# Scatter of expert rows by accumulating DMA, with the routing weights stored beside the gathered rows

## The chip, the cores and the metric

The kernel runs on one core of a Trainium2 chip. The metric is the device time of one execution in microseconds (us), as the median of several runs. The profile comes from one further execution that the hardware profiler recorded. Engines: PE multiplies matrices (PEld is its weight load), DVE, ACT and POOL work on vectors, SP only issues DMAs here; ACT and POOL issue DMAs too.

## What is computed

The input is 8 sequences of 1,024 tokens of 256 values, 8,192 tokens in all. After a layer norm, one branch is a diagonal linear recurrence and the other a mixture of 8 experts, of which each token uses its best two.

```python
xn = _layernorm(x, axis=-1)
# recurrence: h_t = A * h_{t-1} + (xn_t B_w^T + B_b), A = sigmoid(log_A)
s = einsum('btn,dn->btd', h, C_w) + C_b
# experts
logits = einsum('bsh,he->bse', xn, Wr) + br
routing_weights, expert_indices = top_k(logits, 2)
routing_weights = softmax(routing_weights, axis=-1)
c = sum(one_hot(expert_indices, 8) * routing_weights[..., None], axis=-2)
h = silu(einsum('bsh,ehi->besi', xn, W1)) * einsum('bsh,ehi->besi', xn, W3)
y = einsum('besi,eih->besh', h, W2)
g = silu(einsum('bse,besh->bsh', c, y))
out = x + s * g
```

Inputs and result are float32.

## The kernel before

Engines run their own programs and meet at semaphores; the order on each is the order of the code, with no scheduler. There are 64 token tiles of 128 rows (TILES) in 16 chunks of 4 (CHUNKS, CT).

**Head (0 to about 155 us).** SP loads x chunk by chunk (L261). DVE, POOL and ACT normalise, PE transposes, and SP stores the normalised rows to the DRAM tensor xn_rows (L264), one row of 256 floats per token. PE computes router logits. DVE then finds the best two experts of each token (L677 to L683, top2_ready). Meanwhile PE makes the input products of the recurrence, called bx, two halves per chunk (make_bx, L979), and ACT moves each from its PSUM bank to h_sb (keep_bx, L450). There are four banks, so PE's half m of chunk c waits until the half two chunks earlier has been moved: bx_ready >= 2c + m - 3, that is both halves of chunk c-3 and the first of chunk c-2 for m = 0. ACT's program before chunk 3 also holds the sigmoid of log_A (L455) and the exp of the difference of the two logits, called ratio (L457), each with a table load. Between products PE makes ranks (L989, L990), edge transposes (L995), a histogram (L1001) and prefix sums; DVE turns them into slots, and 128 one-hot pairs (L731, L732) are multiplied on PE (L1019) into tables that give for each of 18,176 expert slots its token. The tables become gather_idx and scatter_idx (L749 to L763). DVE also makes weight1 = 1 / (1 + ratio) (L717, L718). SP loads the first expert's weights at the end of chunk 2 (L276), and ACT splits them into a high part from 140 us on (L491).

**Middle (to about 800 us).** 71 tiles of 256 slots, sorted by expert. For each tile POOL gathers 2 x 128 rows of xn_rows by an indirect DMA (L366, a ring of four tiles), PE transposes them (L1036), ACT and DVE split them into a high and a low part (L517, L781), PE multiplies (L1047 to L1049 and L1077, L1078), ACT and DVE do silu, product and splits, ACT copies the low half of y (L531), DVE adds it to the high half (L799), and POOL scatters the 256 rows to y_rows (L373), one row per token and choice, 16,384 rows in all. POOL's program alternates: gather tile i+4, scatter tile i. Slots that hold no token are skipped by an index out of bounds. In the first 32 tiles DVE also runs the recurrence's scans (L840).

**Tail (800 us on).** For each chunk SP loads the rows of the first and of the second choice (L287, two DMAs of 512 KB, a ring of four chunks), DVE mixes them (mix, L880: ratio x second + first), ACT applies silu with the scale weight1 (L586), PE has computed the output states of the chunk into two banks of S_BANKS (L1118 the bias, L1122 the products; four chunks of banks), DVE multiplies (apply, L891) and adds x (add_x, L898), and SP stores (L291). The DVE order is mix(g), apply(g-1), add_x(g-2). SP starts loading when the last scatter has landed.

## Time and profile before

| | us |
|---|---|
| median of 3 runs | 879.77 (879.41 to 879.9) |
| profiled execution | 880.07 |
| its span, first to last instruction | 878.3 |
| mean granted TensorE clock | 0.979 |

Busy shares are means over the whole span; what a stage is worth is read from timelines of that stage. In the timelines of the profile a row has the start, the length, the engine, the line of the kernel, what is written from what, the number of instructions merged into the row, and in brackets the idle time before it with the one that ended it. An engine's name with a q (SPq, ACTq) marks a row of the issuing queue, above all a DMA's issue. Landing is when all of the DMA's completions had arrived. A granted clock of 1.00 is 2.4 GHz, 0.50 is 1.2 GHz.

### The profile page before, as it was taken

The page shows a single profiled execution, that of the slowest core. Times are in us where ns is not written, and L with a number is a line of the kernel's source. Part 1 is how long each engine was busy: PE and PEld are TensorE (multiplying, and loading weights), DVE is VectorE, ACT ScalarE, POOL GpSimd, SP SyncE. Part 2 cuts the span into 40 slices and gives each one's busy share as a digit, 9 for nine tenths or more (in the row PEclk, how much of TensorE's full clock was granted, in tenths as well). Part 3 has the DMA queues.
Part 4 walks back from the last instruction along what each step waited for, and adds up shares of the span by engine and source line. Part 5 has one row for each costly group of instructions (what it writes and reads, how often), then busy time and mean ns, then how long its engine had stood idle before and what let it go on. Part 6 is the DMA issues. An engine that isn't in the chain of part 4 may idle for free.

```text
span 878.3 us, 17926 instructions
## 1 busy us (share of the span) xinstructions
PE 815.5 (93%) x5608; PEld 730.3 (83%) x5608; DVE 521.3 (59%) x1149; ACT 395.5 (45%) x768; POOL 321.5 (37%) x345
## 2 busy tenths in 40 slices
PE   2579994899999999999999999999999999998994
PEld 2444442899999999999999999999999999997883
DVE  5837896446575665655655443545554553543998
ACT  3664674334454443434544443434444543432443
POOL 3420402244444444444453534444444534421000
PEclk9989998899999999999999999999999999999997
DMA  9942002112141321112222311112332211203998
GB/s 297 322 161 72 1 0 75 58 57 65 54 129 51 102 82 60 60 54 66 96 89 81 101 54 60 60 54 75 111 106 79 62 59 60 60 16 110 360 384 296
DMA packets 65982, 90.78 MB, mean 103 GB/s; under 512 B 7646, under 2 KB 53219, under 8 KB 65956
## 3 DMA queue, kind: packets, MB, share of 16 engines
q1 hardware_dynamic: 51092, 54.80, 18.6%
q0 software_dynamic: 13632, 35.41, 12.9%
q10 hardware_dynamic: 1232, 0.28, 0.2%
q8 instruction: 9, 0.15, 0.1%
q14 instruction: 17, 0.14, 0.1%
HBM read 56.90 MB, written 35.39 MB: 105 GB/s over the span
## 4 chain that ended last, share of the span: by engine, by line
PE 87%; DVE 7%; issue 3%; ACT 2%; DMA 1%; DVEq 0%; ACTq 0%
PE bank L1047 16%; PE bank L1049 16%; PE bank L1048 16%; PE bank L1077 15%; PE bank L1078 8%; PE bank L979 5%; PE bank L1122 5%; PE bank L1036 3%; DVE stats L610 2%; PE bank L939 2%; DVE g_sb L880 1%; PE bank L1019 1%; ACT xnT L402 1%; PE bank L949 1%; DVE x_sb L898 1%
## 5 line engine op out<-in xcount | busy, mean ns | idle before, releaser
L1047 PE MATMUL bank<-xh,W_sb 128*128 128x256 f32 x1136 | 322.6, 284 | 3.0 <-DVE xl L781 3.0
L1049 PE MATMUL bank<-xl,W_sb 128*128 128x256 f32 x1136 | 322.1, 284 | 0.0
L1048 PE MATMUL bank<-xh,W_sb 128*128 128x256 f32 x1136 | 322.1, 284 | 0.0
L373 POOL DMA_INDIRECT y_rows<-y_sb,scatter_idx x142 | 145.2, 1022 | 326.0 <-DVE y_sb L799 302.7
L787 DVE TENSOR_TENSOR hbuf<-hbuf,bank 128x512 f32<-128x512 f32 x142 | 97.7, 688 | 239.7 <-PE bank L1049 220.4
L1047 PEld LDWEIGHTS bank<-xh,W_sb 128*128 128x128 f32 x1136 | 216.7, 191 | 6.9 <-issue 3.6
L1049 PEld LDWEIGHTS bank<-xl,W_sb 128*128 128x128 f32 x1136 | 216.7, 191 | 0.0
L1048 PEld LDWEIGHTS bank<-xh,W_sb 128*128 128x128 f32 x1136 | 216.6, 191 | 0.0
L1077 PE MATMUL bank<-W_sb,hh 128*128 128x512 f32 x568 | 207.6, 406 | 0.9 <-DVE y_sb L799 0.9
L366 POOL DMA_INDIRECT xg<-xn_rows,gather_idx x142 | 142.8, 1006 | 89.1 <-DVE scatter_idx L763 45.9
L1078 PE MATMUL bank<-W_sb,hl 128*128 128x256 f32 x568 | 158.5, 279 | 0.0
L527 ACT ACTIVATE hh<-hbuf 128x512 fp32r<-128x512 f32 x142 | 89.0, 627 | 108.2 <-DVE hbuf L787 62.8
L523 ACT ACTIVATE hbuf<-bank 128x512 f32<-128x512 f32 x142 | 84.7, 596 | 105.9 <-PE bank L1049 104.3
L1077 PEld LDWEIGHTS bank<-W_sb,hh 128*128 128x128 f32 x568 | 106.7, 188 | 23.3 <-issue 1.1
L1078 PEld LDWEIGHTS bank<-W_sb,hl 128*128 128x128 f32 x568 | 107.3, 189 | 0.0
L531 ACT ACTIVATE y_low<-bank 128x256 f32<-128x256 f32 x142 | 46.8, 381 | 101.1 <-PE bank L1078 100.8
L792 DVE TENSOR_TENSOR hl<-hbuf,hh 128x512 fp32r<-128x512 f32 x142 | 91.8, 683 | 0.1
L781 DVE TENSOR_TENSOR xl<-bank,xh 128x512 fp32r<-128x512 f32 x71 | 49.1, 692 | 36.0 <-ACT xh L517 22.9
L517 ACT ACTIVATE xh<-bank 128x512 fp32r<-128x512 f32 x71 | 42.4, 598 | 52.8 <-PE bank L1036 40.2
L799 DVE TENSOR_TENSOR y_sb<-bank,y_low 128x256 f32<-128x256 f32 x142 | 52.8, 413 | 21.5 <-ACT y_low L531 20.8
L979 PE MATMUL bank<-xnT,BwT 128*128 128x512 f32 (+1 forms) x128 | 62.8, 609 | 1.2 <-issue 1.2
L1122 PE MATMUL bank<-CwT,h_sb 128*128 128x256 f32 x256 | 62.1, 387 | 0.0
(163 smaller groups left out, 720.1 us busy)
## 6 DMA issues: line engine op xcount, KB each, us to landing
yy<-y_rows SPq DMA_DIRECT2D x32, 512.0 KB, 7.8
raw<-L_ffn_W SPq DMA_DIRECT2D x24, 512.0 KB, 3.6
x_sb<-L_attn_x SPq DMA_DIRECT2D x16, 512.0 KB, 9.0
out<-x_sb SPq DMA_DIRECT2D x16, 512.0 KB, 7.6
xn_rows<-h_sb SPq DMA_DIRECT2D x14, 512.0 KB, 4.8
xg<-xn_rows,gather_idx POOLq DMA_INDIRECT x142
y_rows<-y_sb,scatter_idx POOLq DMA_INDIRECT x142
xn_rows<-scratch SPq DMA_DIRECT2D x2, 512.0 KB, 2.9
```

The source lines that it names most:

```text
L366: eng.indirect_dma_start(out=xg[:, i % XG_RING, t, :], out_offset=None, in_=xn_rows, in_offset=bass.IndirectOffsetOnAxis(ap=gather_idx[:, ...
L373: eng.indirect_dma_start(out=y_rows, out_offset=bass.IndirectOffsetOnAxis(ap=scatter_idx[:, 2 * i + t:2 * i + t + 1], axis=0), in_=y_sb[:, ...
L527: eng.activation(hh[:, r, n * 512:(n + 1) * 512], hbuf[:, n * 512:(n + 1) * 512], ACT.Copy).then_inc(hh_ready, 1)
L787: eng.tensor_tensor(half, half, ps_up[n][:, :], ALU.mult).then_inc(h_ready, 1)
L792: eng.tensor_tensor(hl[:, r, cols], hbuf[:, cols], hh[:, r, cols].bitcast(f32), ALU.subtract).then_inc(hl_ready, 1)
L979: last = eng.matmul(bank[2 * q + m][:, :], BwT[:, k, m * P:(m + 1) * P], xnT[:, bass.ds(c, 1), k, :].rearrange("p a c -> p (a c)"), start= ...
L1047: eng.matmul(part, high, x_h, start=k == 0, stop=False)
L1048: eng.matmul(part, low, x_h, start=False, stop=False)
L1049: last = eng.matmul(part, high, x_l, start=False, stop=k == KD - 1)
L1077: eng.matmul(ps_y[t][:, :], h_h, W_sb[:, at:at + 2 * D], start=k == 0, stop=False)
L1078: last = eng.matmul(ps_y[t][:, 0:D], h_l, W_sb[:, at:at + D], start=False, stop=k == KI - 1)
L1122: last = eng.matmul(o, h_g[:, m, t * P:(t + 1) * P], CwT[:, m * D:(m + 1) * D], start=False, stop=t % 2 == 1 and m == KN - 1)
```

## The change

The routing weights are computed in full in the head: weights[:, :, 0] is 1 / (1 + ratio), weights[:, :, 1] is the second choice's weight minus the first's. xn_rows gets two more columns (ROW = 258), and ACT stores the weights there by one DMA, so that a gather of a token's row brings them along. For each slot DVE computes its weight w_slot from the two columns and a table choice_of, which tells whether the slot is of the first or the second choice. ACT's copy of the low half of y and DVE's addition now multiply by w_slot. The scatter adds (compute_op=ALU.add) into y_rows, which has one row per token and is zeroed first by SP from a zeroed strip of xnT (zero_rows), after POOL's memset; empty slots gather from and scatter to 256 extra rows. As two rows of one token may not be in flight at once, the scatter of a tile waits for the landing of the one before. ACT's first high split and POOL's first gather wait for the zeroing, POOL's first gather also for the weights. In the tail SP issues the loads of all 16 chunks at once, one row per token; the mix is gone, silu runs over a whole chunk, and DVE multiplies and adds by half chunks.

```diff
-    xn_rows = nc.dram_tensor("xn_rows", [T, D], f32).ap()
-    y_rows = nc.dram_tensor("y_rows", [2 * T, D], f32).ap()
+    xn_rows = nc.dram_tensor("xn_rows", [T + TW, ROW], f32).ap()
+    weights_v = xn_rows[0:T, D:ROW].rearrange("(j p) k -> p j k", p=P)
+    y_rows = nc.dram_tensor("y_rows", [T + TW, D], f32).ap()
...
+            def zero_rows():
+                eng.wait_ge(zeros_ready, 1)
+                for n in range(ZERO_PARTS):
+                    j = TILES // ZERO_PARTS
+                    eng.dma_start(y_v[:, n * j:(n + 1) * j, :], zeros[:, 0:D].unsqueeze(1).broadcast_to([P, j, D])).then_inc(rows_zeroed, 16)
+                for rows in (xn_rows, y_rows):
+                    cols = rows.shape[1]
+                    eng.dma_start(rows[T:T + TW, :].rearrange("(t p) d -> p t d", p=P),
+                                  zeros[:, 0:cols].unsqueeze(1).broadcast_to([P, 2, cols])).then_inc(rows_zeroed, 16)
...
+            eng.wait_ge(bx_psum, 2 * 4)
+            eng.memset(zeros, 0.0).then_inc(zeros_ready, 1)
...
             def scatter(i):
                 wait_apart(eng, y_ready, i + 1)
+                if i:
+                    eng.wait_ge(y_stored[(i - 1) % Y_RING], 32 * ((i - 1) // Y_RING + 1))
                 for t in range(2):
                     eng.indirect_dma_start(out=y_rows,
...
-                                           in_=y_sb[:, i % Y_RING, t, :], in_offset=None, bounds_check=2 * T - 1, oob_is_err=False)\
+                                           in_=y_sb[:, i % Y_RING, t, :], in_offset=None, bounds_check=T + TW - 1, oob_is_err=True,
+                                           compute_op=ALU.add)\
...
             for c in range(BX_BEFORE):
+                if c == 2:
+                    eng.wait_ge(top2_ready, 1)
+                    eng.activation(weights[:, :, 1], m2, ACT.Exp).then_inc(ratio_ready, 1)
                 if c == 3:
                     eng.activation(A_sb[:, :], A_sb[:, :], ACT.Sigmoid).then_inc(A_ready, 1)
-                    eng.wait_ge(top2_ready, 1)
-                    eng.activation(ratio[:, :], m2, ACT.Exp).then_inc(ratio_ready, 1)
+                    eng.wait_ge(weights_ready, 1)
+                    eng.dma_start(weights_v, weights[:, :, :], allow_slow_non_contiguous=True).then_inc(w_stored, 16)
...
-            def keep_y_low():
+            def keep_y_low(i):
+                eng.wait_ge(slot_weighed, i + 1)
                 for t in range(2):
-                    eng.activation(y_low[:, t, :], ps_y[t][:, D:2 * D], ACT.Copy).then_inc(y_low_ready, 1)
+                    eng.activation(y_low[:, t, :], ps_y[t][:, D:2 * D], ACT.Identity, scale=w_slot[:, bass.ds(2 * i + t, 1)]).then_inc(y_low_ready, 1)
...
+            for c in range(CHUNKS):
+                eng.wait_ge(y_loaded[c], 16)
+                eng.activation(yy[:, c, :], yy[:, c, :], ACT.Silu).then_inc(g_ready, 1)
...
+            w1, w2 = weights[:, :, 0], weights[:, :, 1]
+            eng.wait_ge(ratio_ready, 1)
+            link(eng.tensor_scalar(w1, w2, 1.0, None, ALU.add))
+            link(eng.reciprocal(w1, w1))
+            link(eng.tensor_tensor(w2, w2, w1, ALU.mult))
+            eng.tensor_tensor(w2, w2, w1, ALU.subtract).then_inc(weights_ready, 1)
             eng.wait_ge(rank_psum, 1)
...
+                for t in range(2):
+                    at = bass.ds(2 * i + t, 1)
+                    last = eng.scalar_tensor_tensor(out=w_slot[:, at], in0=xg[:, q, t, D + 1:D + 2], scalar=choice_of[:, at],
+                                                    in1=xg[:, q, t, D:D + 1], op0=ALU.mult, op1=ALU.add)
+                last.then_inc(slot_weighed, 1)
```

Three places show what moves. In the rows below L numbers are those of the kernel that each fence is of. First ACT's queue in the head, around the products of chunks 0 to 4; before:

```order
L450 ACTIVATE h_sb<-bank,Bb_sb 128x512 [waits xn_stored1,bx_psum]
L450 ACTIVATE h_sb<-bank,Bb_sb 128x512 [waits bx_psum]
L455 ACT_TABLE_LOAD
L455 ACTIVATE A_sb<-A_sb 128x2
L457 ACT_TABLE_LOAD
L457 ACTIVATE ratio<-h_sb 128x64 [waits top2_ready]
L450 ACTIVATE h_sb<-bank,Bb_sb 128x512 [waits bx_psum] x2
L450 ACTIVATE h_sb<-bank,Bb_sb 128x512 [waits xn_stored2,bx_psum]
```

The same place now:

```order
L468 ACT_TABLE_LOAD
L468 ACTIVATE weights<-h_sb 128x64 [waits top2_ready]
L462 ACTIVATE h_sb<-bank,Bb_sb 128x512 [waits xn_stored1,bx_psum]
L462 ACTIVATE h_sb<-bank,Bb_sb 128x512 [waits bx_psum]
L470 ACT_TABLE_LOAD
L470 ACTIVATE A_sb<-A_sb 128x2
L472 DMA xn_rows<-weights 128x64x2 [waits weights_ready]
L462 ACTIVATE h_sb<-bank,Bb_sb 128x512 [waits bx_psum] x2
L462 ACTIVATE h_sb<-bank,Bb_sb 128x512 [waits xn_stored2,bx_psum]
```

The exp stands one chunk earlier, and the issue of the weights' DMA (128 partitions x 64 rows x 2 values) stands between the eviction of chunk 2 and that of chunk 3. Second, POOL from the index tables on; before and now:

```order
L361 CAST tile_first<-scratch 128x71 [waits pool_step]
L366 DMA xg<-xn_rows,gather_idx 128x256 [waits xn_stored4,xn_stored5,xn_stored3,xn_stored6,xn_stored2,xn_stored7,xn_stored1,bx_psum,xn_stored0,tables_ready]
L366 DMA xg<-xn_rows,gather_idx 128x256 x7
L366 DMA xg<-xn_rows,gather_idx 128x256 [waits xT_psum]
L366 DMA xg<-xn_rows,gather_idx 128x256
L373 DMA y_rows<-y_sb,scatter_idx 16384x256 [waits y_ready]
L373 DMA y_rows<-y_sb,scatter_idx 16384x256
```

```order
L369 IOTA scratch 128x142 [waits cum_psum]
L373 DMA xg<-xn_rows,token_idx 128x258 [waits xn_stored5,xn_stored6,xn_stored4,xn_stored7,xn_stored3,rows_zeroed,xn_stored2,bx_psum,xn_stored1,w_stored,xn_stored0,tables_ready]
L373 DMA xg<-xn_rows,token_idx 128x258 x7
L373 DMA xg<-xn_rows,token_idx 128x258 [waits slot_weighed]
L373 DMA xg<-xn_rows,token_idx 128x258
L382 DMA y_rows<-y_sb,token_idx 8448x256 [waits y_ready]
L382 DMA y_rows<-y_sb,token_idx 8448x256
L373 DMA xg<-xn_rows,token_idx 128x258 [waits slot_weighed]
L373 DMA xg<-xn_rows,token_idx 128x258
L382 DMA y_rows<-y_sb,token_idx 8448x256 [waits y_ready,y_stored0]
```

The first gather waits for the weights and the zeroing too, and from the second scatter on each waits for the one before. Third, DVE in the tail now, after the last y:

```order
L887 TENSOR_TENSOR Cb_rows<-Cb_raw,Cb_hi 1x256
L895 TENSOR_TENSOR yy<-yy,bank 128x512 [waits s_psum,g_ready]
L895 TENSOR_TENSOR yy<-yy,bank 128x512 [waits s_psum]
L895 TENSOR_TENSOR yy<-yy,bank 128x512 [waits s_psum,g_ready]
L895 TENSOR_TENSOR yy<-yy,bank 128x512 [waits s_psum]
L901 TENSOR_TENSOR x_sb<-yy,x_sb 128x512 [waits u_ready] x2
```

There is no mix ahead of the multiplications, the second half of a chunk waits for its own bank, and the two half additions of a chunk stand behind the multiplications of the next.

## Rows read from the trace of the kernel before

**Rows 1.** The page, section 1: busy us (share of the span) of each engine.

```profile
PE 815.5 (93%) x5608; PEld 730.3 (83%) x5608; DVE 521.3 (59%) x1149; ACT 395.5 (45%) x768; POOL 321.5 (37%) x345
```

**Rows 2.** Chain that ended last, middle stage: start us, us, what.

```profile
449.86 0.44 PE bank L1036 x4
458.87 0.44 PE bank L1036 x4
```

**Rows 3.** Groups by line, 800 to 878.3 us: busy us, mean ns, idle before.

```profile
L880 DVE SCALAR_TENSOR_TENSOR g_sb<-yy,ratio 128x256 f32<-128x256 f32 x64 | 26.7, 479 | 11.0 <-DMA yy<-y_rows 11.0
L891 DVE TENSOR_TENSOR g_sb<-g_sb,bank 128x512 f32<-128x512 f32 x32 | 20.4, 680 | 0.0
...
L898 DVE TENSOR_TENSOR x_sb<-g_sb,x_sb 128x1024 f32 x12 | 14.6, 1219 | 0.0
```

**Rows 4.** Timeline of the tail: start us, us, engine, line, what [idle before].

```profile
801.98 0.99 POOL L373 DMA_INDIRECT y_rows<-y_sb,scatter_idx  x1 [0.30 <-issue]
...
804.13 16.57 SPq L287 DMA_DIRECT2D yy<-y_rows  x14
...
809.53 1.67 DVE L880 SCALAR_TENSOR_TENSOR g_sb<-yy,ratio 128x256 f32<-128x256 f32 x4 [8.93 <-DMA yy<-y_rows]
...
861.35 1.89 PE L1122 MATMUL bank<-CwT,h_sb 128*128 128x256 f32 x8
...
863.30 1.89 PE L1122 MATMUL bank<-CwT,h_sb 128*128 128x256 f32 x8
...
872.18 2.35 DVE L898 TENSOR_TENSOR x_sb<-g_sb,x_sb 128x1024 f32<-128x1024 f32 x2
```

**Rows 5.** Waits (us, times, longest), then one group by line, 156 to 799 us.

```profile
POOL y_rows L373 <- DVE y_sb L799: 300.6, 70, 17.1
...
L799 DVE TENSOR_TENSOR y_sb<-bank,y_low 128x256 f32<-128x256 f32 x140 | 52.0, 413 | 17.8 <-ACT y_low L531 17.1 <-issue 0.7
```

**Rows 6.** Timeline of the head, DVE and ACT.

```profile
75.82 0.23 DVE L683 TENSOR_TENSOR h_sb<-h_sb 128x64 f32<-128x64 f32 x1
...
77.81 1.28 ACT L455 ACT_TABLE_LOAD   x1
...
78.82 1.53 DVE L689 TENSOR_TENSOR_SCAN scratch<-h_sb,bank 128x64 f32<-128x64 f32 x8 [2.77 <-PE bank L990]
...
80.62 0.26 ACT L457 ACTIVATE ratio<-h_sb 128x64 f32<-128x64 f32 x1
```

**Rows 7.** SP's DMA issues, then packets by queue (q10: ACT's) in 6.6:8.2.

```profile
20.29 1.42 SPq L261 DMA_DIRECT2D x_sb<-L_attn_x  x1
...
59.53 0.36 SPq L264 DMA_DIRECT2D xn_rows<-scratch  x1
...
806.21 0.57 SPq L287 DMA_DIRECT2D yy<-y_rows  x1
806.83 1.35 SPq L287 DMA_DIRECT2D yy<-y_rows  x1
...
q1 hardware_dynamic: 301, 0.31, 64.6%
q10 hardware_dynamic: 232, 0.00, 8.0%
```

**Rows 8.** Timeline of PE, around chunk 5 and at the first expert tile.

```profile
85.92 7.03 PE L979 MATMUL bank<-xnT,BwT 128*128 128x512 f32 x16
...
152.64 0.69 PE L1036 MATMUL bank<-ident,xg 128*128 128x128 f32 x2 [11.27 <-DMA xg<-xn_rows,gather_idx]
```

**Rows 9.** Windows: PE, PEld, DVE, ACT, POOL busy (x), PEclk, DMA share, GB/s.

```profile
10.00:22.00 12.00, 5.47 (x24) 4.71 (x24) 9.26 (x42) 7.91 (x17) 4.97 (x4) 1.00 1.10 353
...
100.00:130.00 30.00, 28.52 (x137) 13.73 (x135) 29.75 (x153) 23.26 (x56) 0.00 (x0) 1.00 0.00 1
...
156.00:159.00 3.00, 3.00 (x16) 3.00 (x15) 0.24 (x1) 0.60 (x1) 2.39 (x3) 0.50 0.63 185
159.00:162.00 3.00, 3.00 (x26) 3.00 (x25) 0.29 (x1) 0.60 (x1) 0.56 (x1) 0.94 0.49 158
```

More of the change, by code:

```diff
@@ L34 @@
 KD = D // P
+ROW = D + 2
 KI = I // P
@@ L848, in _ @@
                     step_and_scan(i0, n, stored=i0 * 16 + (n - 1) // 2 * 32)
-            with loop(eng, 4 * BATCH, EXP_TILES - 3, 2) as i0:
-                for n in range(2):
+            with loop(eng, 4 * BATCH, EXP_TILES - 3, 4) as i0:
+                for n in range(4):
                     expert_step(i0 + n, n, i0 * 16 + (n - 1) // 2 * 32)
@@ L885, in apply @@
-            def apply(g0, q):
-                eng.wait_ge(g_ready, g0 + q + 1)
-                eng.wait_ge(s_psum, g0 + q + 1)
-                for n in range(2):
-                    two = g_sb[:, q, 2 * n:2 * n + 2, :]
-                    last = eng.tensor_tensor(two, two, bank[S_BANKS[q][n]][:, :].rearrange("p (t d) -> p t d", t=2), ALU.mult)
-                last.then_inc(u_ready, 1)
-            def add_x(g0, q):
-                eng.wait_ge(u_ready, g0 + q + 1)
-                x_g = x_sb[:, bass.ds((g0 + q) * CT, CT), :]
-                eng.tensor_tensor(x_g, g_sb[:, q, :, :], x_g, ALU.add).then_inc(out_ready, 1)
@@ L920, in _ @@
+            for c in range(CHUNKS):
+                apply(c)
+                if c:
+                    for n in range(2):
+                        add_x(c - 1, n)
+            for n in range(2):
+                add_x(CHUNKS - 1, n)
         @block.tensor
```

172 lines of the change are left out of this document (72 added, 100 removed).

## The prediction

> **What bounds the kernel now.** I read the page's busy shares first: PE is busy for 93% of the span, DVE for 59%, ACT 45%, POOL 37% [rows 1]. These are means, so three stages were read apart. In the middle (155 to 799 us) PE runs 71 expert tiles, one each 9.0 us (the transposes of two neighbours stand in the chain of work at 449.86 and 458.87 [rows 2]), in step with nothing but itself. In the head PE makes the input products (bx) chunk by chunk, with the routing chain of DVE, PE, POOL and ACT threaded between them. In the tail (800 us on) PE makes two half chunks of output states per chunk, 1.95 us each (861.35 to 863.30 [rows 4]), 3.91 us a chunk; DVE needs 4 x 0.48 (mix), 2 x 0.68 (multiply) and 1.22 (add), which overlap to 3.92 us a chunk [rows 3]. Both are full, but DVE starts later: its first mix waits until 809.53 for y rows, and its last add ends at 874.53, 9.3 us after PE's last product (863.30 + 1.89 = 865.19) [rows 4]. So the tail's end is DVE's, the middle is PE's, and the head is a chain that ACT also stands on.
>
> The profiled execution took 880.07 us with a span of 878.3, so 1.8 lie outside; the median of the runs is 879.77, and both differ by less than the 0.2% (1.8 us) that a measurement can tell.
>
> **The tail.** The mix leaves DVE (16 x 4 x 0.48 = 30.7 us busy) and half of the loads go (8.4 of 16.8 MB). DVE then needs 2 x 0.68 + 2 x 0.61 = 2.6 us per chunk, less than PE's 3.91, so PE becomes the bound. What is late next: PE's last half chunk at 865.2; then DVE's one multiply 0.68 and four half adds (two of them chunk 14's, which now stand behind it) at 0.62 = 2.5; 868.4. Today 3.8 us pass from the last add to the span's end (874.53 to 878.3); I take 3.5 with smaller last stores (an estimate from those 3.8). That gives 871.9. Two things precede it: y_sb's add takes a scalar (0.479 against 0.413 for the two-operand form [rows 3, 5]), and y_low a scale, twice at the last tiles; at most 0.6 in all, so 872.5: **-5.8 us** against 878.3. Cover for the loads: the last scatter was issued at 801.98 and seen by SP at 804.13, the first pair of loads served DVE at 809.53 [rows 4]. PE first needs a freed bank at 800.75 + 4 x 3.91 = 816.4. A single load, one silu (about 1.1) and one multiply fit with over 4 us to spare; a last scatter slower by more than that would cost its excess.
>
> **The middle.** Per tile come two one-column DVE operations, a scalar form in two more, and POOL waits for the landing of the scatter before. POOL issues four indirect DMAs of 1.0 plus 0.3 between them in 9.0 us and stood waiting for y_sb for 300.6 us in 70 waits, 4.3 each [rows 5]. The scatter it must now see landed is a whole tile (9 us) old, where a scatter was seen 2.15 us after its issue [rows 4]. Accumulating is in no row: it can cost nothing to 4.3 us a tile without reaching PE; I take **0**. The gathers, 1,032 bytes for 1,024, run four tiles ahead. DVE's extra 0.5 us per tile lies in the 41% in which it is idle [rows 1].
>
> **The head, small parts.** Four DVE operations on 64 columns now stand before the rank scan, and wait for an exp which ACT runs one chunk earlier. top2 is ready at 75.82 + 0.23 = 76.05; one table load of 1.28 and the exp of 0.26 give 77.6 [rows 6], and the four operations on 64 columns (the exp's own width, and the one at 75.82 takes 0.23 [rows 6]) with the reciprocal about 1.5: 79.1 where the scan began at 78.82 [rows 6]. PE's next product after the slots was ready when PE got there, and the two weight operations removed later give it back: 0. The index chain after the last one-hot is one DVE step shorter and has fewer links: **-0.4**, and with it the first gather. The zeroing writes 8.4 MB from 83 us on; ACT and POOL need it at 140 and 145. At the 353 GB/s of the loads between 10 and 22 us [rows 9] it is 24 us; hidden even at half that rate.
>
> **The head, the part that decides.** At chunk 3 ACT issues one DMA that writes 8,192 pieces of 8 bytes (64 tiles x 128 rows), 512 for each of 16 engines. It stands in ACT's queue ahead of the eviction of chunk 3, and PE's chunk 5 needs that bank. What does an issue cost the issuing engine? SP's issue of a DMA with 512 pieces (32 per engine) took 0.36 us with an empty queue, but 1.42 each in the stream of x loads. In the tail five such issues pass at 0.40 to 0.57 and the sixth is held for 1.35 [rows 7]. So the queue takes some 5 x 32 = 160 pieces per engine, then the issuer stands until pieces have left. If that limit counts pieces, ACT stands until 512 - 160 = 352 per engine are gone. The nearest row for a small piece is the window 6.6 to 8.2 us, with 232 packets of the ACT queue's 4-byte loads [rows 7]: their records fill 8.0% of 16 x 1.6 = 25.6 us, 8.8 ns each; if all that SP's packets (64.6%) leave free is theirs, 9.06 / 232 = 39 ns. So 352 pieces take between 3.1 and 13.7 us alone. From 84 us on zero writes share the engines: 3.3 us alone (some 85 pieces at 39 ns), then 267 x (39 + 46, a 1 KB packet at full rate) = 22.7: 26 in all (46 ns is 1,024 bytes at a sixteenth of 353 GB/s [rows 9]).
> ACT reaches the issue at 77.6 + 2 x 0.69 (chunk 2) + 1.28 + 0.20 = 80.5; pieces move from about 81.7. ACT is free at 84.8 (low), 95.4 (39 ns alone) or 107.7 (shared). The eviction adds 0.7. PE started chunk 5 at 85.92 [rows 8]: so it is late by 0, 10.2 or 22.5 us. I take the middle of the two upper values, 16.3, since zero writes join in but need not alternate one for one. Nothing behind it catches up: PE's chunks 5 and 6, the histogram, the one-hots (DVE busy 29.75 of 30 us between 100 and 130 [rows 9]) and the tables are a chain. After 11.3 us of idle PE started again at 152.64 [rows 8] and still ran at clock 0.50 (1.2 GHz) in 156 to 159, at 0.94 in the next 3 us [rows 9]: some 6.6 us at half speed, 3.3 lost. Total **+19.6**.
>
> The Trainium skill says the same more strictly (Perfetto Trace Analysis, section DMA Instruction — HWDGE): the row of such an issue ends only when all descriptors have been generated, and they don't all fit the buffer. It also says that a strided last dimension becomes one descriptor per element (DMA: Bandwidth & Descriptors, Rules for kernel authors). The rows of SP agree with the first as far as they go; a DMA larger than the buffer is in no row. By the rule ACT stands; without it the sum loses the 19.6.
>
> **Sum.** 880.07 + 19.6 - 5.8 - 0.4 = 893.5.
>
> **Rivals.**
> H, ACT held, as above: 893.5. For it speaks that SP was held again and again at a full queue. Its own range: late by 6 to 32 us with the clock, 880 to 908.
> A, faster: the issue is a command that is accepted at once (the limit of five counts DMAs, not pieces, which these rows can't tell, as all had 512), or small pieces leave at 8.8 ns, so that ACT is free before PE needs it. Then 880.07 - 6.2 = 873.9. It decides at 86 us less the eviction: ACT must be free by about 85.2.
> C, the accumulating DMAs: each of the 142 would have to take over 2.9 us on POOL (4.3 of slack over two, above 1.0) or a landing over a turn; 1 us beyond that per tile is +71, some 945. Nothing in the trace points to a price of three times the plain scatter.
> D, the two cancel: ACT is held until 91 to 93, +6: no change.
>
> **Chances.** H 0.50, A 0.39, C 0.05, D 0.03, other mixtures 0.03. Predicted 893.5, the likeliest. The range takes in A (873.9 less 3, since the tail's and chain's terms may be larger) and H with shared engines: 871 to 908; beyond lie C and the slowest of H, and some of A's edge. Faster by over 0.2% 0.40, within 0.03, slower 0.57.
>
> **What would show it.** ACT's issue row for the weights: over 4 us and PE idle before chunk 5 is H; 0.4 to 0.6 us is A. PE's first expert product at 155.26 + 19 (H) or 155 (A). Tail: PE never waits after 816, DVE ends 3.2 us behind PE, and the loads take one row per chunk. Wrong would be: PE waiting between tiles (C), PE waiting in the tail for a late first load, or the one-hots starting on time although PE was late.

## The result: 868.57 us, faster, outside the range

The changed kernel took 868.57 us (median of 4 runs, 867.06 to 869.86) where the kernel before took 879.84 beside it (4 runs, 879.41 to 880.67): a ratio of 0.9863 [0.9846, 0.988], 1.4% less and clear of the spread. Forecast were 893.5 us, range 871 to 908. The sign was wrong and the time lies 2.4 us below the range. The profiled execution took 868.84 us with a span of 866.8, so 11.5 of span are gone.

Three marks cut both spans (the first state product is that of the bias, L1118 before and L1112 now): PE's first expert product, PE's first product of the output states, and the end.

| | first expert product | first state product | end of span | middle | tail |
|---|---|---|---|---|---|
| before | 155.26 | 800.75 | 878.3 | 645.49 | 77.55 |
| changed | 155.46 | 795.54 | 866.8 | 640.08 | 71.26 |
| difference | +0.2 | | -11.5 | -5.4 | -6.3 |

The head, which was to lose 19, lost 0.2. The tail gained what was forecast. And the middle, for which the forecast says 0, gained 5.4. (The first tile of the middle still runs in part at a granted clock of 0.50 [rows 9] and took 9.64 to 11.07 us in the profiles of this study, so these marks don't tell apart middles that differ by up to 1 us.)

**The head after.** Timeline, 75 to 88 us, of the changed kernel: start us, us, engine, line, what [idle before].

```profile
76.85 0.26 ACT L468 ACTIVATE weights<-h_sb 128x64 f32<-128x64 f32 x1 [0.42 <-DVE h_sb L691]
...
77.38 0.55 DVE L697 RECIPROCAL weights<-weights 128x64 f32<-128x64 f32 x1
...
78.23 0.23 DVE L699 TENSOR_TENSOR weights<-weights 128x64 f32<-128x64 f32 x1
78.49 0.38 ACTq L472 DMA_DIRECT2D xn_rows<-weights  x1
...
79.59 1.53 DVE L703 TENSOR_TENSOR_SCAN scratch<-h_sb,bank 128x64 f32<-128x64 f32 x8 [1.13 <-PE bank L982]
...
81.31 0.69 ACT L462 ACTIVATE h_sb<-bank,Bb_sb 128x512 f32<-128x512 f32 x1 [1.23 <-PE bank L971]
...
83.39 6.72 SPq L279 DMA_DIRECT2D y_rows<-xnT  x2
...
86.69 1.88 PE L971 MATMUL bank<-xnT,BwT 128*128 128x512 f32 x4
```

The fourth row decides. ACT issued the DMA of 8,192 pieces of 8 bytes in 0.38 us and went on to its evictions at 81.31, which answers to the 0.36 of an issue of 32 pieces per engine in [rows 7]. The page gives its landing:

```profile
q10 hardware_dynamic: 9440, 0.34, 1.1%
...
xn_rows<-weights ACTq DMA_DIRECT2D x1, 64.0 KB, 20.5
```

ACT's queue had 1,232 packets before and has 9,440 now, so each 8-byte piece is a packet of its own. The DMA landed 20.5 us after its issue, and nobody stood waiting for it. That is not one price for a piece, though. The packets of ACT's queue in the windows 78 to 86, 78 to 87 and 90 to 94 us:

```profile
q10 hardware_dynamic: 5311, 0.04, 50.8%
```

```profile
q10 hardware_dynamic: 5798, 0.05, 61.4%
```

```profile
q10 hardware_dynamic: 1088, 0.01, 24.5%
```

The first piece moved at 81.7, and 5,311 of the 8,208 packets were through by 86: 4.3 us, 16 engines, 13 ns each (2,082 of them between 84 and 85, 7.7 ns each). Then came the zeroing's 1 KB writes on the same engines: in 90 to 94 a piece took 59 ns of its engine (16 x 4 us / 1,088), and 76 in the mean from 87 to the last piece at 98.4. The forecast's 85 ns beside a zero write was near that; its 39 ns alone was three times too dear.

**The middle after.** The chain of work in the middle, and then the costliest groups by line (busy us, mean ns), PE's two kinds of expert product among them.

```profile
313.15 0.44 PE bank L1028 x4
322.07 0.44 PE bank L1028 x4
```

```profile
L382 POOL DMA_INDIRECT y_rows<-y_sb,token_idx x142 | 230.3, 1622 | 205.1 <-DVE y_sb L811 174.5
L1039 PE MATMUL bank<-xh,W_sb 128*128 128x256 f32 x1136 | 318.2, 280 | 3.0 <-DVE xl L788 3.0
...
L373 POOL DMA_INDIRECT xg<-xn_rows,token_idx x142 | 176.0, 1240 | 87.5 <-DVE token_idx L770 44.5
...
L1070 PE MATMUL bank<-W_sb,hl 128*128 128x256 f32 x568 | 159.6, 281 | 0.0
```

The tile period is 8.92 us where it was 9.01 [rows 2] (before, tiles of 8.96 and of 9.02 us took turns, 8.99 in the mean). PE still waits for nothing. It runs the same 3,408 gate and up products and 1,136 down products as before. Its rows for them were before:

```profile
L1047 PE MATMUL bank<-xh,W_sb 128*128 128x256 f32 x1136 | 322.6, 284 | 3.0 <-DVE xl L781 3.0
L1078 PE MATMUL bank<-W_sb,hl 128*128 128x256 f32 x568 | 158.5, 279 | 0.0
```

The former now read 318.2, 280. The down products did not get quicker but a little dearer (159.6, 281). By their starts, the mean step between gate and up products fell from 119.9 to 117.8 ns, 48 x 71 x 2.1 = 7.1 us less, and the mean step between down products rose from 184.1 to 185.8 ns, 16 x 71 x 1.7 = 1.9 us more: 5.2 of the 5.4 us. So PE is quicker inside one kind of product. A count shows it best; PE's busy time (x instructions), clock, DMA share and GB/s in a stretch of the middle, of before and then of the changed kernel:

```profile
200.00:300.00 100.00, 100.00 (x756) 1.00 0.24 75
```

```profile
200.00:300.00 100.00, 100.00 (x766) 1.00 0.42 80
```

At the same granted clock, busy all the time, PE got through 10 more instructions in 100 us. Busy shares can't show such a thing: 93% before [rows 1], 93% after.

```profile
PE 809.6 (93%) x5608; PEld 723.0 (83%) x5608; DVE 525.1 (61%) x1244; ACT 399.2 (46%) x720; POOL 441.5 (51%) x347
```

POOL went from 321.5 to 441.5 us: the accumulating scatters take 1.55 to 1.62 us each where the plain ones took 1.0, and the gathers' mean rose as well. Its wait for y_sb fell to match, from 300.6 in [rows 5] to:

```profile
POOL y_rows L382 <- DVE y_sb L811: 174.5, 69, 16.5
```

**The tail after.** Timeline of the changed kernel, which answers to [rows 4].

```profile
795.54 0.47 PE L1112 MATMUL bank<-Cb_rows,pick 128*128 128x512 f32 x1 [2.35 <-DVE Cb_rows L887]
...
797.18 1.55 POOL L382 DMA_INDIRECT y_rows<-y_sb,token_idx  x1 [2.93 <-DMA y_rows<-y_sb,token_idx]
799.04 1.55 POOL L382 DMA_INDIRECT y_rows<-y_sb,token_idx  x1 [0.30 <-issue]
802.79 5.72 SPq L306 DMA_DIRECT2D yy<-y_rows  x7
806.87 1.06 ACT L600 ACTIVATE yy<-yy 128x1024 f32<-128x1024 f32 x1 [12.80 <-DMA yy<-y_rows]
807.96 0.69 DVE L895 TENSOR_TENSOR yy<-yy,bank 128x512 f32<-128x512 f32 x1 [12.56 <-ACT yy L600]
...
858.09 1.89 PE L1116 MATMUL bank<-CwT,h_sb 128*128 128x256 f32 x8
...
860.01 0.69 DVE L895 TENSOR_TENSOR yy<-yy,bank 128x512 f32<-128x512 f32 x1 [1.20 <-PE bank L1116]
860.62 2.49 DVE L901 TENSOR_TENSOR x_sb<-yy,x_sb 128x512 f32<-128x512 f32 x4
```

DVE now waits for PE in front of each multiply, and ends 3.1 us behind PE's last product (859.98 to 863.11; it was 9.3). PE has the bound of the tail, with one idle of 2.35 us at its start (2.14 before).

### The profile page after: what moved, and what is told of

The parts are those of the page before. It is cut to its first block, busy times and chain, and to the rows that moved or that the text cites. A ratio compares the mean times of both kernels' runs of the same rounds, so it can differ in the third digit from the quotient of the medians.

```text
span 866.8 us, 18032 instructions
## 1 busy us (share of the span) xinstructions
PE 809.6 (93%) x5608; PEld 723.0 (83%) x5608; DVE 525.1 (61%) x1244; ACT 399.2 (46%) x720; POOL 441.5 (51%) x347
## 3 DMA queue, kind: packets, MB, share of 16 engines
q10 hardware_dynamic: 9440, 0.34, 1.1%
## 4 chain that ended last, share of the span: by engine, by line
PE 91%; DVE 5%; ACT 1%; issue 1%; DMA 1%; DVEq 0%; POOL 0%; ACTq 0%
PE bank L1040 16%; PE bank L1039 16%; PE bank L1069 15%; PE bank L1041 15%; PE bank L1070 8%; PE bank L1116 7%; PE bank L971 6%; PE bank L1028 4%; DVE stats L618 2%; PE bank L931 2%; PE bank L941 1%; PE bank L1112 1%; PE bank L1011 1%; ACT xnT L414 1%; DMA x_sb<-L_attn_x 1%
## 5 line engine op out<-in xcount | busy, mean ns | idle before, releaser
L382 POOL DMA_INDIRECT y_rows<-y_sb,token_idx x142 | 230.3, 1622 | 205.1 <-DVE y_sb L811 174.5
L1039 PE MATMUL bank<-xh,W_sb 128*128 128x256 f32 x1136 | 318.2, 280 | 3.0 <-DVE xl L788 3.0
L1040 PE MATMUL bank<-xh,W_sb 128*128 128x256 f32 x1136 | 318.7, 281 | 0.0
L1041 PE MATMUL bank<-xl,W_sb 128*128 128x256 f32 x1136 | 317.7, 280 | 0.0
L373 POOL DMA_INDIRECT xg<-xn_rows,token_idx x142 | 176.0, 1240 | 87.5 <-DVE token_idx L770 44.5
L1039 PEld LDWEIGHTS bank<-xh,W_sb 128*128 128x128 f32 x1136 | 214.3, 189 | 6.8 <-issue 3.6
L1040 PEld LDWEIGHTS bank<-xh,W_sb 128*128 128x128 f32 x1136 | 213.9, 188 | 0.0
L1041 PEld LDWEIGHTS bank<-xl,W_sb 128*128 128x128 f32 x1136 | 213.1, 188 | 0.0
L1070 PE MATMUL bank<-W_sb,hl 128*128 128x256 f32 x568 | 159.6, 281 | 0.0
L548 ACT ACTIVATE y_low<-bank,w_slot 128x256 f32<-128x256 f32 x142 | 59.7, 472 | 120.2 <-PE bank L1070 112.9
L811 DVE SCALAR_TENSOR_TENSOR y_sb<-bank,w_slot,y_low 128x256 f32<-128x256 f32 x142 | 61.4, 474 | 29.7 <-ACT y_low L548 28.8
```

Of the source, the lines that this page charges most:

```text
L373: eng.indirect_dma_start(out=xg[:, i % XG_RING, t, :], out_offset=None, in_=xn_rows, in_offset=bass.IndirectOffsetOnAxis(ap=token_idx[:, 2 ...
L382: eng.indirect_dma_start(out=y_rows, out_offset=bass.IndirectOffsetOnAxis(ap=token_idx[:, 2 * i + t:2 * i + t + 1], axis=0), in_=y_sb[:, i ...
L1039: eng.matmul(part, high, x_h, start=k == 0, stop=False)
L1040: eng.matmul(part, low, x_h, start=False, stop=False)
L1041: last = eng.matmul(part, high, x_l, start=False, stop=k == KD - 1)
L1070: last = eng.matmul(ps_y[t][:, 0:D], h_l, W_sb[:, at:at + D], start=False, stop=k == KI - 1)
```

## Experiments

The first four were run together, the next four together, and so on; each batch had its own runs of the kernel before (medians 880.15, 880.8, 880.6, 880.9 and 880.78, 878.9 to 883.2 in all its runs but a stray one of 4,544). The batches were on different chips: e1 to e4 and e12 to e15 on one, e5 to e8, e9 to e11, and e16 and e17 on three more. The kernel before agrees on all of them; a comparison across batches (e10 with e8 above all) also compares chips.

The rows had shown that the programs of PE differ in nothing in the middle. What does differ is where its operands lie: a row of xg grew from 256 to 258 elements, 4 x 2 x 2 x 4 = 64 bytes for the ring, and whatever is allocated behind xg starts 64 bytes later in each partition (xh, then xl, hbuf, hh, hl). W_sb stays. That gave a theory, P, with an edit of one line.

**Place alone, and twice the shift.**

```diff
--- before (e1) and changed kernel (e2), the same line in both
+            pad_xh = sb("pad_xh", [P, 16], f32, mid)
             xh = sb("xh", [P, KD * TW], f32r, mid)
```

> The kernel before, with 64 unused bytes per partition between xg and xh and nothing else, so that xh and the tiles behind it lie 64 bytes later, as they do in the changed kernel, whose xg rows have two more columns (4 tiles x 2 x 2 values = 64 bytes). Open question: in the changed kernel the stretch from the first expert product to the tail takes 640.1 us, before it took 645.5, although PE's instructions are the same. Theory P (the place of xh and xl in SBUF sets the pace of the products that read them): the products of L1047 to L1049 start every 0.118 us instead of 0.120, and the kernel takes 5.4 us less, 874.4. Rival Q (the pace changes with the other engines' work or the DMA traffic of the changed kernel): 879.8, no change.

Measured: 874.04 (873.33 to 875.18), ratio 0.9924 [0.991, 0.9938]; period 8.91, middle 640.29, head and tail as before. Sixty-four unused bytes in the old kernel give 5.2 of the 5.4 us. Nothing else of the change has a part in it that can be told from the spread.

> The changed kernel with 64 more unused bytes ahead of xh, which then begins at a multiple of 128 bytes again, as before the change, but 128 bytes later. Theory P with an alignment of 128 bytes: the loss comes back, 868.6 + 5.4 = 874.0, and the products start every 0.120 us. P with something other than that alignment: 868.6. Q: 868.6.

Measured: 871.09 (870.46 to 871.6), period 8.95, middle 642.65. It lies between the two: half of the gain is given back at 128 bytes.

**Is the place periodic?** The same with 192 bytes in front, so that xh lies 256 behind.

```diff
+            pad_xh = sb("pad_xh", [P, 48], f32, mid)
             xh = sb("xh", [P, KD * TW], f32r, mid)
```

> The changed kernel with 192 unused bytes ahead of xh, which then begins 256 bytes behind its place of before (the changed kernel has it 64 behind, e2 had it 128 behind, 871.1). Period of a tile in the middle so far: 9.01 us at 0, 8.92 at 64, 8.95 at 128. Theory P1 (the pace repeats every 256 bytes or less): 9.01 again, 868.6 + 71 x 0.09 = 875. Rival P2 (only the place of before is bad): 8.92 to 8.95, 868.6 to 871.

Measured: 874.19 (873.29 to 876.03), ratio 0.9931 [0.991, 0.9951]; period 9.02. That is the changed kernel without its gain in the middle, to 0.2 us of 868.57 + 5.4: the slow place comes back at 256 bytes. PE's row reads again as before the change:

```profile
L1040 PE MATMUL bank<-xh,W_sb 128*128 128x256 f32 x1136 | 322.9, 284 | 3.0 <-DVE xl L789 3.0
```

**The tail alone.** The kernel before with the new tail: one y row per token, all loads issued at once, no mix, half adds. In short:

```diff
-            yy = sb("yy", [P, YY_RING, 2, CT, D], f32, tail)
-            g_sb = sb("g_sb", [P, YY_RING, CT, D], f32, tail)
+            yy = sb("yy", [P, CHUNKS, CT * D], f32, tail)
...
-            for q in range(YY_RING):
-                load_y(q, q)
+            for c in range(CHUNKS):
+                eng.dma_start(yy[:, c, :].rearrange("p (t d) -> p t d", t=CT), y_v[:, 0, c * CT:(c + 1) * CT, :]).then_inc(y_loaded[c], 16)
```

> The kernel before with the new tail alone: one y row per token (the first choice's, unweighted), loads of all 16 chunks at once, silu over a chunk, products and additions by half chunks. It leaves out the second choice's rows and the weights. Theory T (the tail was DVE's and is now PE's, and that part is worth what the two traces show, 77.6 to 71.3 us from PE's first state product to the end): 879.8 - 6.3 = 873.5. Rival U (part of the tail's gain comes from the other edits, the accumulation or the place of tiles): less than 4 us, above 875.8.

Measured: 873.84 (873.32 to 874.12), ratio 0.9923 [0.9908, 0.9938]; tail 71.24, middle 645.78 with tiles as before. With e1 the account closes to 1 us: e1 is 6.1 and e4 6.3 below 880.15, together 867.7, and 868.57 was measured.

**The DMA of the weights in two parts.** If its issue doesn't stand, does the next one?

```diff
-                    eng.dma_start(weights_v, weights[:, :, :], allow_slow_non_contiguous=True).then_inc(w_stored, 16)
+                    for j0, j1 in ((0, TILES - 4), (TILES - 4, TILES)):
+                        eng.dma_start(weights_v[:, j0:j1, :], weights[:, j0:j1, :], allow_slow_non_contiguous=True).then_inc(w_stored, 16)
```

> The changed kernel with the weights' DMA cut in two on ACT's queue, 60 tiles (480 pieces of 8 bytes for each of 16 engines) and behind it 4 tiles (32 each). The one DMA of 512 pieces per engine did not hold ACT (its issue took 0.38 us) and landed after 20.5 us. Theory R (an issue into an empty queue is taken whatever its size, the next one stands until the earlier pieces are nearly gone): the second issue is held for some 13 to 17 us, ACT is free at about 93 to 96, PE's chunk 5 starts 7 to 10 us late, with the clock's loss 876 to 882 in all. Rival S (the limit counts DMAs, some five of them): both issues take 0.4 us, 868.6.

Measured: 874.23 median (870.61 the profiled run, the others 873.8 to 874.9), ratio 0.9931 [0.9916, 0.9946]. Timeline of this kernel:

```profile
78.03 8.87 ACTq L473 DMA_DIRECT2D xn_rows<-weights  x1
...
86.94 1.84 ACT L462 ACTIVATE h_sb<-bank,Bb_sb 128x512 f32<-128x512 f32 x3 [7.74 <-issue]
...
87.68 1.13 PE L972 MATMUL bank<-xnT,BwT 128*128 128x512 f32 x2 [1.70 <-ACT h_sb L462]
```

The second issue, of 32 pieces per engine, stood for 8.87 us, which is neither R's 13 to 17 nor S's 0.4. This is the scene that the prediction painted: ACT late, the eviction at 86.94, PE waiting 1.70 us for its bank at 87.68, and the first expert product at 157.03 for 155.46. The hold that I had given to the large DMA falls on whichever issue comes behind it. In the profiled run 1.6 us of the head and 868.6 of span follow from it; the other three runs are 3 to 4 us above the profiled one, and no trace shows why.

> The changed kernel with the weights' DMA cut in two the other way round: 4 tiles first (32 pieces per engine), 60 tiles (480) behind. In e3, with the large one first, the second issue was held for 8.87 us. Theory R1 (an issue that doesn't find the queue empty stands until its own pieces fit, some 140 per engine): the second issue is held for about (512 - 142) x 0.037 = 13.7 us plus 1, ACT is free at about 93, PE's chunk 5 starts some 7 us late, 876 to 880. Rival R2 (an issue stands only until the DMA ahead of it has been taken up, whatever its own size): both issues take 0.4 to 0.5 us, and the kernel takes 868.6.

The edit is the same with `((0, 4), (4, TILES))`. Measured: 867.59 (867.21 to 867.93); the issues took 0.38 and 0.53 us.

> The changed kernel with the DMA of the weights in two equal halves (256 pieces of 8 bytes for each engine, twice). G: the queue holds a fixed number of pieces per engine and a DMA larger than that is written into it while it empties; with 60 tiles ahead of 4 the second issue stood 8.87 us behind 480 pieces, which at 36 ns is some 190 moved and 290 left. Then a first half of 256 fits whole, and the second issue takes under 1 us. F: the issue behind stands for a share of the time that the DMA ahead takes (8.87 of about 17.3 us, one half): then the second issue takes 4 to 5 us. L: it stands until about 160 pieces are left, as the x loads do, with 36 ns: (256 - 160) x 0.036 = 3.5 us and the 2 us start, 5 to 6 us. Time by G 868 to 869; by F and L ACT is free at 83.4 to 84.5, still ahead of PE's need, 868 to 870 too: the issue row decides, not the time.

Measured: 867.05 (one run). The second issue:

```profile
77.65 6.71 ACTq L473 DMA_DIRECT2D xn_rows<-weights  x1
```

None of the three numbers was met. With 32, 256 and 480 pieces per engine ahead of it the second issue took 0.53, 6.71 and 8.87 us. Its own size (480, 256, 32) doesn't decide, since the largest passed at once; what lies ahead does, but not as a fixed number of pieces, since 256 would then have passed by G. When the second issue ended, all 4,096 pieces ahead of it had moved in e9 (4,101 packets of the queue by 84.36), and all but some 100 per engine in e3 (6,022 by 86.9); in e5 it ended before any had. ACT's next eviction at 84.4 was still in time, as expected of the time. SP's second to fourth zero DMAs (128 pieces per engine ahead of each) also stood 6 to 7 us each, with no one behind them in need until 140.

**What the accumulation costs.**

```diff
-                                           in_=y_sb[:, i % Y_RING, t, :], in_offset=None, bounds_check=T + TW - 1, oob_is_err=True,
-                                           compute_op=ALU.add)\
+                                           in_=y_sb[:, i % Y_RING, t, :], in_offset=None, bounds_check=T + TW - 1, oob_is_err=True)\
```

> The changed kernel whose scatter writes instead of adding; the wait for the landing of the scatter before is kept. It leaves out the sum of a token's two expert rows. POOL's scatter instructions took 1.62 us in the changed kernel against 1.02 before. Theory V (adding costs only hidden time: 0.6 us per instruction on POOL and some us ahead of the first load of the tail): the time stays at 868.6 within 1 us, POOL's scatters take about 1.0 us and the first load is issued 2 to 3 us earlier. Rival W (the adding DMAs disturb the middle, for instance through SBUF or the queues): the middle is faster by over 1 us.

Measured: 867.23 (867.12 to 869.02). Groups of this kernel and its wait for y_sb:

```profile
L382 POOL DMA_INDIRECT y_rows<-y_sb,token_idx x142 | 146.0, 1028 | 318.1 <-DVE y_sb L810 294.8
L373 POOL DMA_INDIRECT xg<-xn_rows,token_idx x142 | 145.6, 1025 | 87.8 <-DVE token_idx L769 44.6
```

Without the addition the scatter is back at 1.03 us and the gather at 1.03 (1.24 beside accumulating scatters), POOL waits 294.8 us for y_sb as it did before the change, and the time is 1.3 us lower. The spans differ by 1.4: the tail is 1.7 shorter and the middle 1.0 longer (641.12 for 640.08), at the same 8.92 us a tile; the first tile, at the low clock, took 10.89 for 9.64. The tail's part is PE's clock too, at 1.2 GHz in the first half chunks of the changed kernel and at 2.4 here, after the same idle of 2.35 us. The window 798 to 800 us (PE busy, PEclk, DMA share, GB/s) of the changed kernel and then of this one:

```profile
798.00:800.00 2.00, 2.00 (x6) 0.50 0.38 41
```

```profile
798.00:800.00 2.00, 2.00 (x11) 1.00 0.19 66
```

So 115 us of work on POOL cost nothing that can be told from the spread.

**The idle at the tail's start.** PE waited 2.35 us for the bias rows (Cb_rows), which DVE makes behind the last y add though they need nothing of it.

```diff
             expert_step(last, 0, 16 * (last - 2), gate=False, xT=False)
-            add_y(last, 0, 16 * last)
...
                 eng.tensor_tensor(Cb_rows[low, n * D:(n + 1) * D], Cb_raw[low, :], Cb_hi[low, :].bitcast(f32), ALU.subtract).then_inc(Cb_ready, 1)
+            add_y(last, 0, 16 * last)
```

> The changed kernel with DVE's two operations on Cb_rows ahead of the last addition of y instead of behind it. In the changed kernel PE stands idle for 2.35 us after the last expert product until these are done, and its first 16 state products then take 4.93 us instead of 3.46. Theory X (with PE the bound of the tail, its start decides): PE starts at about 793.2 and goes on at full clock, 2.3 + 1.5 = 3.8 us less, 864.8. Rival Y (DVE or the first y load is late instead, since the load is issued at 802.8 whatever PE does, and PE then waits for banks): less than 1.5 us, above 867.

Measured: 865.3 (864.65 to 867.58), ratio 0.9839 [0.9821, 0.9857]. PE goes from the last down product straight on, and the clock stays at 1.00 (796 to 804 us), so that the tail is 69.89:

```profile
793.09 0.28 PE L1070 MATMUL bank<-W_sb,hl 128*128 128x256 f32 x1
793.21 0.40 PE L1112 MATMUL bank<-Cb_rows,pick 128*128 128x512 f32 x1
793.45 1.89 PE L1116 MATMUL bank<-CwT,h_sb 128*128 128x256 f32 x8
```

This beats the changed kernel by 3.3 us by an edit of the order alone, so the next runs start from it.

**More places.** The same pad line, sized for xh to lie 192 and 96 bytes behind the old place.

> The kernel with the token output bias ahead of the last y add, with 128 bytes kept free ahead of xh, so that xh, xl and what lies behind start 192 bytes behind a multiple of 256 counted from the old kernel (64 in the changed one). M, the pace depends on the distance to the old place in either direction: 192 is 64 ahead of the next old place, so tiles at 8.92 us and 865 to 866. N, each step of 64 behind costs a bit more, up to the old pace at 256: at 192 tiles at 8.98, 869 to 870. Z, only the place of 64 is fast: 9.01, 871 to 872.

Measured: **852.23** (850.83 to 852.51), ratio 0.9669 [0.9649, 0.9689]: the fastest kernel of this study, 13 us ahead of e8 by 128 unused bytes (on another chip; the kernel before differs by 0.2 us between the two). None of the three theories had that; they all took 64 for the best place. PE's rows, the chain, and the count of its instructions in the same stretch:

```profile
L1040 PE MATMUL bank<-xh,W_sb 128*128 128x256 f32 x1136 | 315.6, 278 | 3.0 <-DVE xl L789 3.0
L1042 PE MATMUL bank<-xl,W_sb 128*128 128x256 f32 x1136 | 315.1, 277 | 0.0
```

```profile
442.65 0.44 PE bank L1029 x4
451.34 0.44 PE bank L1029 x4
460.07 0.44 PE bank L1029 x4
```

```profile
200.00:300.00 100.00, 100.00 (x781) 1.00 0.43 84
```

781 instructions for 766 and 756. Tiles of 8.69 and 8.73 us take turns.

> The same with 32 bytes kept free, 96 bytes behind the old place. N, the pace falls off from 64 to 128: tiles between 8.92 and 8.95, 866 to 867. S, what counts is a step of 32 (a start at an odd multiple of 32 is different in kind from 64 and 128): a period outside 8.92 to 8.95, in either direction.

Measured: 869.81 (869.05 to 870.38), period 8.98: dearer than at 64 and at 128, so N falls and S holds.

> The fastest kernel so far (bias early, xh 192 bytes behind the old place, 852.2) with 32 bytes more: 224 behind. F, 192 is in the middle of a fast region: tiles at 8.7 to 8.8, 852 to 857. O, 192 is one place and odd multiples of 32 behave as 96 did: 8.95 to 9.0, 868 to 871.

Measured: 864.51 (863.79 to 865.32), period 8.90.

> The same with 32 bytes less: 160 behind, between 128 (8.95) and 192 (8.73). F: 8.75 to 8.9, 854 to 864. O: 8.95 to 9.0, 868 to 871.

Measured: 866.03 (865.2 to 866.54), period 8.94. There is no fast region around 192, and no rule by odd multiples of 32 either.

**Whose place?** In the kernel before: xh and xl 192 behind with hbuf and the rest 256 behind; then hbuf and the rest 192 behind with xh and xl where they were.

```diff
--- e12
+            pad_xh = sb("pad_xh", [P, 48], f32, mid)
             xh = sb("xh", [P, KD * TW], f32r, mid)
             xl = sb("xl", [P, KD * TW], f32r, mid)
+            pad_h = sb("pad_h", [P, 16], f32, mid)
             hbuf = sb("hbuf", [P, KI * TW], f32, mid)
--- e13: pad_h alone, with [P, 48]
```

> The kernel before with 192 bytes kept free ahead of xh and 64 ahead of hbuf: xh and xl start 192 bytes behind their old places, hbuf, hh and hl 256 behind theirs, which repeats the old ones if the pace repeats within 256 bytes. X, it is the place of xh and xl that PE reads in the gate and up products: tiles at 8.73 us in place of 9.01, 880.2 - 71 x 0.28 = 860. H, it is the place of the hidden rows (DVE and ACT write them while PE reads xh): 880. B, both: between 862 and 878.

Measured: 872.25 median of 862.04, 871.69, 872.81 and 873.87, ratio 0.9876 [0.981, 0.9943]; period 8.86 in the profiled run (871.69).

> The kernel before with 192 bytes kept free ahead of hbuf alone: xh and xl at their old places, hbuf, hh, hl, y_sb and y_low 192 bytes behind. X: 880, tiles at 9.01. H: 860, tiles at 8.73. B: the rest of what the run with only xh and xl moved leaves of 20 us.

Measured: 880.77 (880.12 to 883.07, 10 runs), ratio 1.0003 [0.9993, 1.0012]; period 8.99. It is xh and xl whose place counts, the columns that PE reads against the weights in the gate and up products; what DVE and ACT write beside it does not on its own.

> The changed kernel with 128 bytes kept free ahead of xh (192 behind the old place, as all that lies behind it). K, the place sets the pace and the kernel doesn't: tiles at 8.73 us, 868.6 - 71 x 0.19 = 855. V, the pace off the old place varies with the kernel and the run: anything from 855 to 868, with a spread of several us between runs.

Measured: 865.53, 865.29, 855.7 and 854.84, ratio 0.9745 [0.9684, 0.9807]; the profiled run was the first, period 8.91.

> The kernel before with 192 bytes kept free ahead of xh and nothing between xl and hbuf, so that all behind moves by 192 too. G, the hidden rows have to move along: tiles at 8.73 us and 860 to 861 in all runs. V: as with xh and xl alone, 862 to 874 with a spread between runs. If both this and the changed kernel with 192 come steady at 8.73, the place decides and 256 for the hidden rows was what cost the other run its pace.

Measured: 863.21 (861.84 to 866.69), ratio 0.9802 [0.9768, 0.9835]; period 8.73. The last two together are V's outcome for the changed kernel: one and the same program ran at 855 twice and at 865 twice. G can't be held either, since e12 once ran at 862.04 with the hidden rows left at 256.

The traces show that the two speeds are not a matter of the run. In e16's profiled run they stand side by side within one execution:

```profile
206.31 0.44 PE bank L1029 x4
215.04 0.44 PE bank L1029 x4
223.96 0.44 PE bank L1029 x4
232.87 0.44 PE bank L1029 x4
```

These are tiles of 8.73, 8.92 and 8.91 us, and from 232.87 on every fourth is one of 8.73 and the other three are of 8.91, to the end of the middle. Inside the short tiles the gate and up products start every 0.1139 us, inside the long ones every 0.1177, at the same granted clock of 1.00. In e12's profiled run the tiles took 8.87 and 8.91 us by turns for most of the middle, and then changed for good:

```profile
695.95 0.44 PE bank L1038 x4
704.81 0.44 PE bank L1038 x4
713.52 0.44 PE bank L1038 x4
```

From 704.81 on each takes 8.71. So at 192 the same products from the same place have at least two paces, and a run's time tells how many tiles had which: all of them the quick one in the traces of e10 and e17 (there with three longer tiles of 9.81, 8.98 and 9.05 us), one in four in e16, the last nine in e12. By that an e16 with quick tiles alone would take 868.57 - 71 x 0.19 = 855, as two of its runs did. A difference between chips doesn't explain a change within one execution; what makes it is open.

All places side by side; the spacing of the products is a mean over 14 tiles of each profile, the period the median of the tiles that the chain of work names. Those of e12 and e16 are mixtures of the two paces.

| xh behind the old place | kernels | us between gate/up products | tile, us | runs, us |
|---|---|---|---|---|
| 0 | before; e13 | 0.1199; 0.1199 | 9.01; 8.99 | 878.9 to 883.2 |
| 64 | changed; e1 | 0.1178; 0.1178 | 8.92; 8.91 | 867.1 to 869.9; 873.3 to 875.2 |
| 96 | e11 | 0.1200 | 8.98 | 869.1 to 870.4 |
| 128 | e2 | 0.1187 | 8.95 | 870.5 to 871.6 |
| 160 | e15 | 0.1180 | 8.94 | 865.2 to 866.5 |
| 192 | e10; e17; e12; e16 | 0.1137; 0.1141; 0.1175; 0.1171 | 8.73; 8.73; 8.86; 8.91 | 850.8 to 852.5; 861.8 to 866.7; 862.0 to 873.9; 854.8 to 865.5 |
| 224 | e14 | 0.1185 | 8.90 | 863.8 to 865.3 |
| 256 | e6 | 0.1199 | 9.02 | 873.3 to 876.0 |

(Different rows hold different kernels, so the runs compare only within a kind: before, e1, e12, e13, e17 have the old tail; changed, e2, e6, e16 the new one; e8, e10, e11, e14, e15 the new one with the bias early.)

## Why the prediction was wrong, step by step

**What bounds the kernel: right, and not used.** The middle was PE's, in step with nothing but itself. From that I concluded that nothing there could change, since PE's instructions were the same. What follows from a stage that only PE bounds is the opposite: each ns per product counts 3,408 times. 0.0021 us less (0.1199 to 0.1178) on 48 products a tile is 0.10 a tile; the down products took 0.03 of it back, and 5.4 us in all were measured. This is the term that is in no part of the sum; it was put at nothing without a reason, and with it the forecast of rival A, 873.9, would have been 868.5.

**The head, the step that failed:** "If that limit counts pieces, ACT stands until 512 - 160 = 352 per engine are gone." The issue took 0.38 us. What the rows had shown was that an issue stands when other DMAs are queued ahead of it, five of 32 pieces per engine; the rule for a DMA that is itself large was drawn from that, and the text said that a DMA larger than the buffer is in no row. The runs show that an issue is not held for its own size when little is queued ahead (512 in 0.38 us, 480 behind 32 in 0.53), and that the one behind a large one is (8.87 and 6.71 us).

The price in this step was wrong as well. With 5,311 packets through by 86 and 5,798 by 87, the 352 pieces per engine (5,632) for which ACT was to stand were gone at some 86.7, where the forecast had 95.4 to 107.7 and only its lowest case 84.8. So even an ACT held by the forecast's own rule would have made PE's chunk 5 late by 1 to 2 us and not by 16.3 (an estimate from these packets; e3, held until 86.90, made PE wait 1.70). Rival A's second reason, small pieces that leave at 8.8 ns, was nearer the truth than its price in H. Sound was the rest: the eviction that waits behind ACT's issue, PE's bank behind that, and 1.6 us later at the first expert product, so nothing that caught up (e3).

The Trainium skill has the row of such an issue end only when all descriptors have been generated (Perfetto Trace Analysis, section DMA Instruction — HWDGE). The trace doesn't show the generating. It shows that the row ended at 78.87, 2.8 us before the first piece moved, so that the hold which I read out of that sentence for the DMA itself did not come; the measurement decides. The other page that I named, one descriptor per element for a strided last dimension (DMA: Bandwidth & Descriptors, Rules for kernel authors), is not put to the test: the last dimension here is two neighbouring values, and each pair went as one packet (8,208 packets more on ACT's queue, not 16,384).

Also the place of the issue in time was off: ACT issued at 78.49, ahead of its table load, not at 80.5. The first piece moved at 81.7 all the same, as forecast, 3.2 us behind its issue where 1.2 had been reckoned; the two errors cancel by luck. The share of 0.50 for H against 0.39 for A rested on one row type of one size; an even split or less was all that it could carry.

**The head, small parts: right in size, wrong by 0.6.** The exp came at 76.85 (77.6 less its own 0.26 was forecast, 0.5 later), the scan at 79.59 for 79.1, 0.8 later than before. The -0.4 of the index chain didn't show; PE's first expert product is at +0.2. Zeroing took from 83.39 to about 116 (last issue 108.98, 7.1 us to its landing): 33 us for the 24 forecast, hidden as said.

**The middle's other terms: right.** The accumulating scatter costs 1.6 for 1.0 us of POOL, "nothing to 4.3 us a tile without reaching PE" held, and e7 bounds it. Only the last one reached anything: it waited 2.93 us for the landing of the one before (797.18), so the first silu started at 806.87 (803.67 in e7). PE first needed a bank later than that, as said.

**The tail: right.** -6.3 (and -6.3 in e4 by itself) for -5.8; DVE's end 3.1 us behind PE for 3.2, the silu 1.06 for about 1.1, 3.7 us from the last add to the end for 3.5. The forecast had PE start the tail where the middle ends; its idle at the start, 2.35 us, was 2.14 before. By the clock after that idle the tail came out at 71.2 or at 69.6 (e7) with the same instructions, which no term of mine held.

**The range.** Its lower end was A's 873.9 less 3. That covers errors in the terms that were named and nothing for a term that was not. With the middle's effect left out, a head like A's lands outside whatever the chances.

## What to carry to other kernels

Where one engine has a stage to itself, the price of its commonest instruction is a term of the sum, and an edit that only shifts what is allocated behind it (here a ring grown by 64 bytes) can move that price: compare instructions finished in a fixed stretch, since the busy share stays 93%. Put a few dozen to some hundred unused bytes ahead of the operand that PE streams, and try several sizes and several runs of each; here that was worth up to 13 us, twice as much as taking 31 us of work off DVE. Look at single tiles too, since a mean can hide two paces. Here a DMA of many small pieces was harmless to the engine that issued it when nothing was issued on that queue soon after; a hold is to be looked for at the next issue, so the small one goes first. And a price per piece read beside other traffic is not its price alone: 13 ns and then 76 ns in one and the same DMA.

## What was not expected of the hardware

**The place of the streamed operand.** The same products, at the granted clock 1.00, start every 0.1199 us with xh at its old place or 256 bytes behind it, in every profile of that kind, and every 0.1137 to 0.1200 at six places between. W_sb stays put in all of them, so the distance to the weights moves along with the place (it was 32,768 bytes, a multiple of 256, in the kernel before); these runs don't separate the two. At 192 bytes the products have two paces, 0.1139 and 0.1177 us, that change from tile to tile within one execution (e16, e12), and one program's runs lie 10 us apart. Whether accesses collide and which, what changes the pace, and whether e10's four runs at 851 to 852 would stay there in more runs, is open.

**The hold of an issue.** 0.53, 6.71 and 8.87 us behind 32, 256 and 480 small pieces per engine; 6 to 7 us behind 128 pieces of 1 KB. When the held issue ended, none of the pieces ahead were left in e9 and some 100 per engine in e3. The rule that gives all of this is open.

**The price of accumulating in DRAM.** An indirect scatter of 128 rows of 1 KB takes POOL 1.6 us with the addition and 1.03 without, and the gathers between them 1.24 for 1.03.
